# A decoder layer on one core: the first attention's projections and the shared gate and up as three products of high and low parts

## The reference

```python
def layer(x, ctx):                       # x 32x128x128, ctx 32x128x96, all float32
    x = x + attention(layernorm(x))      # sigmoid(q), sigmoid(k), per-head k^T v; then
                                         # relu((ln(attn) * (h + beta)) @ Wo + bo)
    x = x + cross(layernorm(x), ctx)     # 16 heads of 64, softmax, @ Wo + bo
    x = x + ffn(layernorm(x))            # shared swiglu + one routed expert of 8
    return x

def attention(x):                        # the products that the change touches
    h = x @ Wh + bh
    q = sigmoid(x @ Wq + bq)
    k = sigmoid(x @ Wk + bk)
    v = x @ Wv + bv
    ...

def ffn(x):
    logits = x @ gate_w                  # top-1 routing
    shared = (silu(x @ sh_gate) * (x @ sh_up)) @ sh_down      # sh_gate, sh_up 128x256
    ...
```

## Time and profile before

| | |
|---|---|
| median of 3 runs | 675.24 us (674.36 to 675.88) |
| the profiled execution, its own time | 674.81 us |
| its span in the trace | 673.1 us |
| mean granted TensorE clock | 0.977 |
| PE busy | 616.9 us, 92% of the span |
| PEld, DVE, ACT, POOL busy | 500.3, 418.2, 417.9, 308.2 us |

### The profile page before, as it was taken

How to read it: one execution, slowest core, us unless ns; L and a number is a source line. 1 busy time by engine, 2 the same in 40 slices (tenths; PEclk the granted TensorE clock), 3 DMA queues, 4 the chain that set the end, 5 groups by cost and what they waited for, 6 DMA issues and landing times.

```text
span 673.1 us, 14742 instructions
## 1 busy us (share of the span) xinstructions
PE 616.9 (92%) x5159; PEld 500.3 (74%) x5159; DVE 418.2 (62%) x1168; ACT 417.9 (62%) x1499; POOL 308.2 (46%) x331
## 2 busy tenths in 40 slices
PE   3578999999998999999999999999999979899993
PEld 1467888878797879787987798779877867566662
DVE  3668655866576657665866586648655446377562
ACT  2338688667765776677666766677666666344551
POOL 3424543345346433743284328432733345146653
PEclk9779999999999999999999999999999999799998
DMA  6200100010001000200010000000000002625420
GB/s 185 72 18 1 28 2 2 1 29 1 1 10 52 1 1 1 60 2 1 1 61 2 1 1 33 1 1 2 32 1 1 2 33 76 223 67 162 134 78 12
DMA packets 24952, 23.48 MB, mean 35 GB/s; under 512 B 7007, under 2 KB 22497, under 8 KB 24880
## 3 DMA queue, kind: packets, MB, share of 16 engines
q1 hardware_dynamic: 20368, 14.91, 8.0%
q0 software_dynamic: 2784, 6.32, 2.6%
q10 hardware_dynamic: 1728, 1.32, 0.7%
HBM read 15.03 MB, written 7.95 MB: 34 GB/s over the span
## 4 chain that ended last, share of the span: by engine, by line
PE 59%; DVE 13%; POOL 10%; issue 9%; ACT 8%; DMA 1%; POOLq 0%; DVEq 0%
PE bank L1178 7%; PE bank L1210 7%; PE bank L1188 5%; PE bank L1199 5%; PE bank L1215 5%; PE bank L1293 5%; ACT prob L977 4%; PE bank L1216 4%; PE bank L1217 4%; POOL routed L518 4%; PE bank L1138 3%; PE bank L1081 3%; POOL prob L526 3%; PE bank L1318 2%; DVE mneg L768 2%
## 5 line engine op out<-in xcount | busy, mean ns | idle before, releaser
L977 ACT ACTIVATE prob<-bank,mneg 128x128 f32<-128x128 f32 x512 | 182.7, 381 | 99.6 <-DVE mneg L768 99.5
L526 POOL TENSOR_TENSOR prob<-prob,rden 128x512 f32<-128x512 f32 x128 | 130.7, 1042 | 173.7 <-DVE rden L775 173.6
L977 ACT ACTIVATION_READ_ACCUMULATOR prob<-bank,mneg 128x1 f32 x512 | 112.4, 220 | 0.0
L983 ACT COPY probT<-bank 128x512 f32<-128x512 f32 x128 | 77.0, 602 | 49.6 <-PE bank L1188 49.0
L768 DVE TENSOR_REDUCE mneg<-bank 128x4 f32<-128x512 f32 x128 | 81.3, 677 | 29.0 <-PE bank L1178 29.0
L1188 PE MATMUL bank<-ident,prob 128*128 128x128 f32 x512 | 78.6, 276 | 3.0 <-POOL prob L526 2.9
L1178 PE MATMUL bank<-kT,qT 64*128 64x128 f32 x1024 | 75.1, 286 | 5.8 <-ACT qT L993 2.4
L1178 PEld LDWEIGHTS bank<-kT,qT 64*128 64x128 f32 x1024 | 63.0, 189 | 18.1 <-issue 12.9
L1188 PEld LDWEIGHTS bank<-ident,prob 128*128 128x128 f32 x512 | 60.4, 142 | 19.2 <-issue 17.0
L1199 PE MATMUL bank<-probT,V 128*64 128x128 f32 x1024 | 71.3, 282 | 0.0
L467 POOL TENSOR_TENSOR rstd<-var_eps,neg_half 128x4 f32<-128x4 f32 x24 | 24.4, 1018 | 96.0 <-DVE var_eps L619 96.0
(11 more groups left out here) (176 smaller groups left out, 1301.8 us busy)
## 6 DMA issues: line engine op xcount, KB each, us to landing
prob<-routed SPq DMA_DIRECT2D x39, 128.5 KB, 2.2
xin<-in_x_dram SPq DMA_DIRECT2D x8, 256.0 KB, 3.2
ctx_nat<-in_ctx_dram SPq DMA_DIRECT2D x8, 192.0 KB, 3.7
routed<-blank ACTq DMA_DIRECT2D x8, 128.5 KB
qT<-in_L_ffn_rt_gate_dram SPq DMA_DIRECT2D x1, 1024.0 KB, 6.9
qT<-in_L_ffn_rt_up_dram SPq DMA_DIRECT2D x1, 1024.0 KB, 9.0
out_dram<-probT,prob POOLq DMA_INDIRECT x39, 2.7
prob<-in_L_xattn_Wq_dram SPq DMA_DIRECT2D x1, 512.0 KB, 6.7
```

Of the source, the lines that this page charges most:

```text
L526: nc.gpsimd.tensor_tensor(view, view, spread(rden[:, m % 2, c * NC:(c + 1) * NC], 2, S), ALU.mult)\
L977: last = nc.scalar.activation(prob[:, m % 2, p * S:(p + 1) * S], bank[c % 2][:, i * S:(i + 1) * S], ACT.Exp, bias=mneg[:, m % 2, p:p + 1], ...
L983: nc.scalar.copy(probT[:, m % 2, c * 512:(c + 1) * 512], made(r1, ("T", m, c))[:])\
```

## The change

All nine float32 products of a group that are named above (four of 384 columns, q, and four of gate and up) become `product3`. `xnT` becomes `xnT_hi` (ACT) and `xnT_lo` (DVE, new step "x^T low"); `h3T` stays for the logits, and `h3T_hi` (a second copy on ACT, ahead of it) and `h3T_lo` (DVE, new step "h^T low") come to it. The banks of "turn x" and "turn h" are now emptied by DVE's subtraction. The weights land in `x2`, which is free at that time, and are split once: `wkvh` and `wq` at the very start, `sh_gu` at n = -1. To make room, `x1n` is now `xn`, `gT` is `qsT`, the tanh is written straight into `act3`, `ctx_nat` has one buffer for two (SP issues the load of a group's context after the group before has been turned), and `x1b` two for three.

```diff
-        wq = sb("wq", [P, D])
-        wkvh = sb("wkvh", [P, 3 * D])
+        wq_hi = sb("wq_hi", [P, D], F32R)
+        wq_lo = sb("wq_lo", [P, D], F32R)
+        wkvh_hi = sb("wkvh_hi", [P, 3 * D], F32R)
+        wkvh_lo = sb("wkvh_lo", [P, 3 * D], F32R)
...
+        x1n = xn
+        gT = qsT
+        raw = x2[:].rearrange("p a b n -> p (a b n)")
+        rawkvh, rawq1, rawgu = raw[:, 0:3 * D], raw[:, 3 * D:4 * D], raw[:, 4 * D:4 * D + 2 * I]
...
-        DVE_S1 = {(0, 0): "stats of x", (0, 3): "first pair", (1, 0): "second pair", (1, 2): "mask",
+        DVE_S1 = {(0, 0): "stats of x", (0, 2): "x^T low", (0, 3): "first pair", (1, 0): "second pair", (1, 2): "mask",
...
-        DVE_F = {(0, 3): "normalise", (1, 1): "route", (1, 2): "activate 0", (1, 3): "rows",
+        DVE_F = {(0, 3): "normalise", (1, 0): "h^T low", (1, 1): "route", (1, 2): "activate 0", (1, 3): "rows",
...
-        S1_BANKS = {"turn x": [(0, "act")], "project first pair": [(1, "dve"), (2, "dve")],
+        S1_BANKS = {"turn x": [(0, "dve")], "project first pair": [(1, "dve"), (2, "dve")],
...
-        F_BANKS = {"turn h": [("h", "act")], "logits": [("l", "dve")],
+        F_BANKS = {"turn h": [("h", "dve")], "logits": [("l", "dve")],
...
                         normalise_first(xn, xin[:, 0], 0)
+                        dve.wait_ge(w1_hi, 1)
+                        nc.vector.tensor_tensor(wkvh_lo[:], rawkvh, wkvh_hi[:].bitcast(F32), ALU.subtract)
+                        nc.vector.tensor_tensor(wq_lo[:], rawq1, wq_hi[:].bitcast(F32), ALU.subtract)\
+                            .then_inc(w1_lo, 1)
+                if step == "x^T low":
+                    ps = made(r2, (g, 0))
+                    dve.wait_ge(xT_hi, g + 1)
+                    nc.vector.tensor_tensor(xnT_lo[:], ps[:], xnT_hi[:].bitcast(F32), ALU.subtract)\
+                        .then_inc(r2.emptied["dve"], 1)
...
+                if step == "h^T low":
+                    ps = made(r2, (g, "h"))
+                    dve.wait_ge(h3_hi, g + 1)
+                    nc.vector.tensor_tensor(h3T_lo[:], ps[:], h3T_hi[:].bitcast(F32), ALU.subtract)\
+                        .then_inc(r2.emptied["dve"], 1)
...
+                    if (n, b) == (-1, 3):
+                        dve.wait_ge(wm_hi, 1)
+                        nc.vector.tensor_tensor(sh_gu_lo[:], rawgu, sh_gu_hi[:].bitcast(F32), ALU.subtract)\
+                            .then_inc(wm_lo, 1)
...
-                    nc.scalar.copy(xnT[:], made(r2, (g, 0))[:]).then_inc(r2.emptied["act"], 1)
+                    nc.scalar.copy(xnT_hi[:], made(r2, (g, 0))[:]).then_inc(xT_hi, 1)
...
-                    nc.scalar.copy(h3T[:], made(r2, (g, "h"))[:]).then_inc(r2.emptied["act"], 1)
+                    nc.scalar.copy(h3T_hi[:], made(r2, (g, "h"))[:])
+                    nc.scalar.copy(h3T[:], r2.bank((g, "h"))[:]).then_inc(h3_hi, 1)
...
+            act.wait_ge(w_in, 16 * 5)
+            nc.scalar.copy(wkvh_hi[:], rawkvh)
+            nc.scalar.copy(wq_hi[:], rawq1).then_inc(w1_hi, 1)
...
+                    if (n, b) == (-1, 2):
+                        act.wait_ge(wm_in, 16 * 4)
+                        nc.scalar.copy(sh_gu_hi[:], rawgu).then_inc(wm_hi, 1)
...
+            def product3(ps, w_hi_, w_lo_, t_hi, t_lo):
+                pe.matmul(ps, w_hi_, t_hi, start=True, stop=False)
+                pe.matmul(ps, w_hi_, t_lo, start=False, stop=False)
+                return pe.matmul(ps, w_lo_, t_hi, start=False, stop=True)
...
-                        pe.matmul(ps[:, 0:3 * D], xnT[:, (u - 1) * S:u * S], wkvh[:], start=True, stop=True)\
-                            .then_inc(r2.ready, 1)
+                        product3(ps[:, 0:3 * D], xnT_hi[:, (u - 1) * S:u * S], xnT_lo[:, (u - 1) * S:u * S], wkvh_hi[:],
+                                 wkvh_lo[:]).then_inc(r2.ready, 1)
...
-                    pe.matmul(claim(r2, (g, 5))[:], wq[:], xnT[:], start=True, stop=True).then_inc(r2.ready, 1)
+                    product3(claim(r2, (g, 5))[:], wq_hi[:], wq_lo[:], xnT_hi[:], xnT_lo[:]).then_inc(r2.ready, 1)
...
-                        pe.matmul(claim(r2, (g, name))[:], sh_gu[:, c0:c0 + P], h3T[:], start=True, stop=True)\
-                            .then_inc(r2.ready, 1)
+                        product3(claim(r2, (g, name))[:], sh_gu_hi[:, c0:c0 + P], sh_gu_lo[:, c0:c0 + P], h3T_hi[:],
+                                 h3T_lo[:]).then_inc(r2.ready, 1)
```

More of the change, by code:

```diff
@@ L114, in decoder_layer @@
         xin = sb("xin", [P, 2, GB, D])
-        ctx_nat = sb("ctx_nat", [P, 2, GB, DE])
+        ctx_nat = sb("ctx_nat", [P, GB, DE])
         ctxT_hi = sb("ctxT_hi", [DE, 2, GB * S], F32R)
@@ L119, in decoder_layer @@
         xn2T_lo = sb("xn2T_lo", [P, 2, GB * S], F32R)
-        x1b = sb("x1b", [P, 3, GB, D])
+        x1b = sb("x1b", [P, 2, GB, D])
         xn = sb("xn", [P, GB, D])
-        xnT = sb("xnT", [P, GB * S])
+        xnT_hi = sb("xnT_hi", [P, GB * S], F32R)
+        xnT_lo = sb("xnT_lo", [P, GB * S], F32R)
         qsT = sb("qsT", [P, GB * S])
@@ L130, in decoder_layer @@
         hb = sb("hb", [P, GB, D])
-        gT = sb("gT", [P, GB * S])
         x1 = sb("x1", [P, GB, D])
-        x1n = sb("x1n", [P, GB, D])
         stats = sb("stats", [P, 3, GB, 6])
@@ L149, in decoder_layer @@
         gate = sb("gate", [P, E])
-        sh_gu = sb("sh_gu", [P, 2 * I])
+        sh_gu_hi = sb("sh_gu_hi", [P, 2 * I], F32R)
+        sh_gu_lo = sb("sh_gu_lo", [P, 2 * I], F32R)
         sh_dn = sb("sh_dn", [P, I // P, D])
@@ L226, in decoder_layer @@
         x_in = [sem("x_landed_even"), sem("x_landed_odd")]
-        c_in = [sem("ctx_landed_even"), sem("ctx_landed_odd")]
+        c_in = sem("ctx_landed")
         consts = sem("constants_ready")
+        w1_hi = sem("s1_weights_high_part")
+        w1_lo = sem("s1_weights_low_part")
+        wm_hi = sem("ffn_weights_high_part")
+        wm_lo = sem("ffn_weights_low_part")
+        xT_hi = sem("xT_high_part")
+        h3_hi = sem("ffn_input_high_part")
         w_hi = sem("cross_weights_high_part")
@@ L317, in decoder_layer @@
         ACT_TAIL = {4: ["copy h^T"], 6: ["score", "tanh 0"], 8: ["tanh 1"]}
-        DVE_TAIL = {3: ["normalise"], 6: ["route", "activate 0"], 7: ["rows"], 8: ["activate 1"], 10: ["shared"]}
+        DVE_TAIL = {3: ["normalise"], 4: ["h^T low"], 6: ["route", "activate 0"], 7: ["rows"], 8: ["activate 1"], 10: ["shared"]}
         POOL_TAIL = {2: ["rstd"], 7: ["record"], 10: ["scatter 0"], 11: ["scatter 1"], 12: ["scatter 2"],
@@ L421, in _ @@
             sp.dma_start(routed[E * REGION:E * REGION + P, :], blank[:]).then_inc(blank_in, 16)
-            for g in range(2, NG):
-                sp.wait_ge(x1_in, g - 1)
-                load_x(g)
-                sp.wait_ge(*r2.made((g - 2, 13)))
+            for g in range(1, NG):
+                sp.wait_ge(*r2.made((g - 1, 13)))
                 load_ctx(g)
+                if g + 1 < NG:
+                    sp.wait_ge(x1_in, g)
+                    load_x(g + 1)
             sp.wait_ge(s_ready, 4 * B)
@@ L495, in s1 @@
                     pool.wait_ge(x1_in, g + 1)
-                    nc.gpsimd.tensor_tensor(x1b[:, g % 3], x1[:], spread(xbo_bc[:], 1, GB), ALU.add)\
+                    nc.gpsimd.tensor_tensor(x1b[:, g % 2], x1[:], spread(xbo_bc[:], 1, GB), ALU.add)\
                         .then_inc(x1b_in, 1)
@@ L791, in residual @@
                 dve.wait_ge(x1b_in, g + 1)
-                nc.vector.tensor_tensor(x2[:, g % 2, b, :], ps[:, 0:D], x1b[:, g % 3, b, :], ALU.add)\
+                nc.vector.tensor_tensor(x2[:, g % 2, b, :], ps[:, 0:D], x1b[:, g % 2, b, :], ALU.add)\
                     .then_inc(r1.emptied["dve"], 1)
@@ L970, in ffn @@
                     ps = made(r2, (g, f"g{k}"))
-                    nc.scalar.activation(tanh3[:], ps[:], ACT.Tanh, scale=0.5).then_inc(tanh_in, 1)
+                    nc.scalar.activation(act3[:, k, :], ps[:], ACT.Tanh, scale=0.5).then_inc(tanh_in, 1)
             def exp_chunk(m, c):
@@ L1115, in s1 @@
                 if step == "turn context":
-                    pe.wait_ge(c_in[g % 2], 16 * (g // 2 + 1))
-                    turned(g, 13, ctx_nat[:, g % 2], DE)
+                    pe.wait_ge(c_in, 16 * (g + 1))
+                    turned(g, 13, ctx_nat, DE)
                 if step == "turn x1":
@@ L1212, in out_product @@
                 last.then_inc(r1.ready, 1)
-            def product3(ps, w_hi_, w_lo_, t_hi, t_lo):
-                pe.matmul(ps, w_hi_, t_hi, start=True, stop=False)
-                pe.matmul(ps, w_hi_, t_lo, start=False, stop=False)
-                return pe.matmul(ps, w_lo_, t_hi, start=False, stop=True)
             def make_qk(part, pair, i):
```

26 lines of the change are left out of this document (13 added, 13 removed).

## The result

| | us, median (runs) | range |
|---|---|---|
| before, same set of runs as the changed kernel | 675.11 (4) | 674.36 to 675.88 |
| changed kernel | 669.62 (4) | 669.36 to 670.19 |
| predicted | 670.2 | 666.0 to 674.5 |

The ratio is 0.9907, with a 95% interval of 0.9883 to 0.993: the change makes the kernel 0.9% faster. The profiled execution of the changed kernel took 670.19 us, its span is 668.5, against 673.1 before.

A forecast was written before the change was run, and what follows sets the result against it. The prediction took PE as the bound, its pieces end to end on the chain of waits. Gains of 6.7 us less costs of 0.3, 0.3, 0.4, 0.5 and 0.2 gave 5.0, so 670.2 us from 675.24; range 666 to 674.5.

The forecast's parts named there:

- Prices: Float32r matmul on PE: 0.175 us for 384 columns, 0.23 for 512; each product gives back 0.115 or 0.16.
- Groups 3 to 7: First attention with gate and up 1 and q: 0.80 us saved a group, 4.0 for five, partly limited by a bank wait.
- Gate and up 1 of groups 5 and 6: These gate and up products in the loop: 0.32 us saved each, 0.65 together.
- Gate and up 0: Groups 0 to 5: first product's saving lost waiting for x1^T's low part; second saves 0.16 us, six times 0.96.
- Turn h: Groups 0 to 6: second ACT copy and DVE subtraction nearly covered; 0.05 us charged each, 0.3 together.
- The start: Before the first projections: weight and x^T splits make PE start later, partly regained; 0.4 us lost.
- Group 1's first pair: On the chain of waits, DVE's subtraction goes between ACT's copy and PE: 0.5 us lost net.
- Split of sh_gu: Gate and up weights: ACT's copy hidden, DVE's 0.69 us has 0.51 of idle time; 0.2 us lost.
- Tail: Group 7's feed-forward: three products save 0.16 us each, 0.48; the uncovered h^T copies cost 0.3.
- the loop of row maxima: Rival, 10%: the loop of DVE, ACT and scores ends last once PE is shorter; 674.4 us, no change.
- weight loads: Rival, 4%: the 72 added loads on PE cost 0.10 us each, 7.2 in all; 677.4 us, slower.
- h^T's low part: Rival, 9%: in turn h it delays DVE's routing and row maxima; at 1.5 us late, 678 us, slower.

The follow-up runs named there:

- four: Changed kernel with a fourth matmul, low by low, in each of the nine new products: 686.07 us, ratio 1.0075 to the kernel before.
- att_only: Kernel before with three-matmul products in the first attention's projections and q alone, feed-forward unchanged: 679.43 us, ratio 0.9981.
- g0_f32: Changed kernel with the first product of gate and up 0 back as one f32 product: 667.83 us, one run.
- before_delay: Kernel before with an idle ACT copy and an idle DVE subtraction where the changed kernel splits the gate and up weights: 678.74 us, ratio 0.9977.
- ffn_only: Kernel before with three-matmul products in gate and up alone, first attention unchanged: 676.92 us, ratio 0.9935.
- after_again: Changed kernel run again, unedited, in a further set: 675.0 us, ratio 0.9927 to the kernel before.
- x1_first: Changed kernel with x1's turn before probabilities times V on PE, and x1^T's high part before oT's copy on ACT: 666.44 us, ratio 0.9866.
- logits_wait: Changed kernel with ACT copying the f32 h^T first and the logits waiting for that copy alone: 668.0 us, one run.
- best: Changed kernel with the edits of both x1_first and logits_wait: 666.56 us, ratio 0.9866 to the kernel before.
- early: Changed kernel with the split of the gate and up weights two passes earlier: 676.64 us, ratio 0.9941 to the kernel before.
- early_tail: As early, with the last group's logits, h^T low and all behind them one tile later in the tail: 676.54 us, ratio 0.9953.

## Why the prediction was right

In the loop the time came out of the mechanism that was forecast, place by place (5.93 us predicted, 5.99 measured). That the whole came within 0.6 us (670.2 predicted, 669.62 measured) is luck: a clock effect that the prediction lacks, a tail term with the wrong sign and a late landing of x nearly cancelled.

- **Prices.** Right: 0.17 to 0.18 for 384 columns, 0.23 for 512. In four an added matmul costs that wherever PE is what ends last.
- **Groups 3 to 7.** 0.80 each predicted; 0.23 + 0.61 = 0.84 measured in 15 and 16 and their like. The first pair comes off in full, its low part hidden; the second pair is cut by the bank wait (att_only: 0.29 for pair and q, where 0.26 was counted).
- **Group 2:** 0.62 predicted, 0.23 + 0.37 = 0.60 measured. **Gate and up 1 of groups 5 and 6:** 0.65 predicted, 0.31 + 0.17 = 0.48 measured (halves 56 and 61). In group 6 the second product starts 0.97 us behind the first instead of 0.70.
- **Gate and up 0:** 0.16 in each of six halves, the first product for nothing. Measured 0.165, and g0_f32 shows the first product's share to be zero.
- **Turn h:** 0.3 charged, 0 measured. The cover of 0.2 us was enough. In its place one half (35) of the changed kernel is 0.34 longer than its like, and the one behind it 0.07 shorter.
- **Together** halves 6 to 62: 5.93 predicted, 5.99 measured.
- **The start:** 0.4 predicted, 0.36 in the first pair of profiles and 1.05 in the second, with 7.30 and 8.51 us for one and the same start in before and before_delay. The term is neither confirmed nor refuted.
- **Group 1's first pair:** 0.5 predicted, 0.56 measured (from group 1's turn of x to the first scores, 3.38 against 2.82). Of "second pair and q save nothing", half 0 is 0.39 shorter and half 1 0.32 longer in att_only, so 0.07 in all: right.
- **Ahead of the turn of x:** 1.0 us later in this profile, with the later landing of x. The second profiles show it to be scatter.
- **Split of sh_gu:** the term "DVE's 0.69 has 0.51 us of idle time before L659, which is on the chain: 0.2" was mis-sized and misread. It costs 0.5 in half 1 and gives 0.5 back in half 2 (before_delay, ffn_only), so nothing (in the changed kernel as in these two, half 1 is longer and half 2 shorter by 0.5 than in att_only). The prediction read one idle time and didn't follow the chain into the next half, where PE's wait ahead of the scores was 1.72 us long.
- **The clock near 66 us:** missing from the prediction. The page's row of clocks before has slices at 7 there only in the start and the tail; the 3.4 us at the lower level are spread over two slices and leave no digit below 9. They cost halves 3 and 4 1.5 us, and in every run with the split, or the idle pair, in pass -1 (changed kernel, after_again, ffn_only, four, before_delay, g0_f32, x1_first, logits_wait, best) they are gone.
- **Tail:** the term 3 x 0.16 less 0.3 = 0.18 gained was mis-sized. From tile 2 to tile 10 it took 21.83 against 21.42, 0.4 lost. The prediction charged the copies and not that the logits wait for DVE's subtraction too, since the bank of h^T is freed by DVE now: logits_wait takes that wait away and the 0.65 with it. The three products did give back 0.17 (tiles 3 to 4) and 0.32 (tiles 5 to 6), the 0.48 that was counted; but 0.26 of it is lost again from tile 6 to 7, where PE then waits 0.17 us for DVE's V, so the copies' term of 0.3 is what was mis-sized: 0.65 + 0.26 = 0.91. Another 0.8 lies ahead of the tail's first tile, 24.08 us from half 63 on against 23.30, where runs of one kernel differ by more (22.11 and 23.30 for the kernel before).

By the ledger, then, against the sum of -5.0: +1.0 ahead of the turn of x, -1.8 in halves 0 to 5 (1.5 of it the clock, 0.2 the split's term), +1.2 behind half 63 (1.03 instead of -0.18), and -0.1 in the loop. Of the rivals, the loop of row maxima did not take over (the halves gave all that PE gave), weight loads did not show, and h^T's low part did not hold up DVE in the loop.

What stays open: why the clock fell after PE's pause of 1.72 us in the kernel before (twice) and in att_only, and not in early and early_tail after a pause of 1.72 us. before_delay shows that two idle instructions are enough to remove the stretch. They shorten the pause to 1.47 us and also move it; which of the two counts is not shown, and by early and early_tail the length alone doesn't decide.

## What to carry to other kernels

A saving on the busiest engine comes through where the chain of waits has that engine's pieces end to end, and is nothing in front of a wait for a bank; it could be told apart half by half to 0.05 us. Price a delay not by the idle time in front of it alone but up to the next long wait on the engine that matters: here 0.5 us went in and came out again one half later. When the engine that frees a buffer is changed, look for everyone who waits for the buffer to be free and means "my copy is ready".

## What the runs showed of the hardware

- **A loop repeats far better than a kernel.** Halves 6 to 62 (472 us) took 471.95, 472.00, 472.06, 471.93 and 471.99 us in five profiles (changed kernel twice, early, early_tail, g0_f32), in three sets of runs. The rest behind half 63 took 105.4 to 115.8. From tile 10 to tile 38 all eight profiles of the first two further sets took 52.0 to 54.6 us, and those of the third set, on the chip of the second, 47.8 to 48.0, as the first profiles of before and of the changed kernel (47.9 and 47.7). The excess stands in a few tiles between 9 and 18; the windows of after_again, then of the changed kernel's first run:

```profile
612.00:620.00 8.00, 5.34 (x20) 3.11 (x20) 3.22 (x9) 2.52 (x9) 4.30 (x5) 0.79 0.35 123
```

```profile
612.00:620.00 8.00, 8.00 (x45) 5.25 (x44) 4.71 (x14) 4.46 (x15) 6.01 (x7) 1.00 0.47 153
```

  In six of the eight a stretch at the lower clock follows; in before_delay and four the granted clock stays at 1.00 there (7.89 of 12.00 us PE busy in before_delay, from 615 us on), so the lower clock isn't what makes the tiles longer. Their cause is open.
- **Work added can keep the clock up.** Two idle instructions of 0.7 us made the kernel before 0.23% faster (0.9977 [0.9964 to 0.9989]); 3.4 us at a granted clock of 0.50 are gone, and halves 3 and 4 are 1.52 us shorter.
- **A half of one kernel can be 0.35 us longer at one fixed place.** Half 35 takes 7.38 to 7.40 instead of 7.04 in all nine profiles of kernels that have both parts of the change, and 7.03 to 7.05 in the five others; att_only has it in halves 21 and 60 instead. It goes with the program and not with the run; the trace shows DVE idle for 0.50 us in front of its reciprocal at L804, with nothing new to wait for that the profile shows. The row of DVE's timeline:

```profile
331.45 0.20 DVE L804 RECIPROCAL rden<-den 128x8 f32<-128x8 f32 x1 [0.50 <-DVE record L790]
```
